# A reordered prologue: zero products, weights split in pieces, four combinations side by side

## The reference

```
mod = (silu(c) @ wmod).reshape(4, 6, 1, 512)      # sa, ca, ga, sb, cb, gb
h   = layernorm(x) * (1 + ca) + sa
q   = h @ Wq.T                                    # 32 heads of 128
k_r = h @ Wkr.T                                   # rotary part of the keys, 8 heads
c_kv = h @ Wdk.T                                  # 512 wide
k_c, v = c_kv @ Wupk.T, c_kv @ Wupv.T             # the keys' rest and the values
q, k = rope(q), rope(k)
x   = x + ga * (softmax(mask(q k^T / sqrt(128))) v @ Wo.T)
h   = layernorm(x) * (1 + cb) + sb
x   = x + gb * (h * w_sum + w_top8 @ expert_bias) # router softmax, best 8 of 64
```

## Time and profile before

| | |
|---|---|
| median of 3 runs | 1451.65 us (1451.25 to 1452.85) |
| profiled execution | 1450.45 us, span in the profile 1449.2 us |
| TensorE | busy 1428.9 us, 99% |
| VectorE | busy 1152.3 us, 80% |
| POOL | busy 1023.7 us, 71% |
| ScalarE | busy 1009.4 us, 70% |

### The profile page before, as it was taken

One profiled execution on the slowest core, in us unless ns is written; L12 is line 12 of the kernel. 1 busy time (PEld: TensorE's weight loads), 2 busy tenths in 40 slices (PEclk: granted clock), 3 DMA queues, 4 the chain that ended last, 5 costly groups with the idle time before them and its releaser, 6 DMA issues.

```text
span 1449.2 us, 24714 instructions
## 1 busy us (share of the span) xinstructions
PE 1428.9 (99%) x7150; PEld 1209.3 (83%) x7150; DVE 1152.3 (80%) x3542; ACT 1009.4 (70%) x2391; POOL 1023.7 (71%) x805
## 2 busy tenths in 40 slices
PE   7999999999999999999999999999999999999997
PEld 7888888888888888888888888888888888888886
DVE  6697777777777777778777777777879989988876
ACT  5687767667767666676777677676667676776674
POOL 3777877667767666776767687667588888886662
PEclk9999999999999999999999999999999999999999
DMA  9488668766766876686588658759888889889871
GB/s 321 152 248 257 211 179 228 223 213 185 209 208 197 229 202 211 189 246 178 170 229 243 205 182 225 191 161 268 238 234 265 262 286 281 265 267 268 270 233 61
DMA packets 215158, 322.05 MB, mean 222 GB/s; under 512 B 42512, under 2 KB 132464, under 8 KB 215024
## 3 DMA queue, kind: packets, MB, share of 16 engines
q1 hardware_dynamic: 214736, 320.39, 74.1%
q10 hardware_dynamic: 288, 0.07, 0.0%
HBM read 179.43 MB, written 140.95 MB: 221 GB/s over the span
## 4 chain that ended last, share of the span: by engine, by line
PE 87%; DVE 5%; POOL 3%; DMA 2%; issue 2%; ACT 1%; SPq 0%; DVEq 0%; ACTq 0%
PE bank_s L642 22%; PE bank_o L804 22%; PE bank_pv L766 14%; PE bank_s L708 13%; PE bank_s L674 6%; PE bank_s L659 5%; PE bank_s L705 1%; PE bank_s L704 1%; POOL PT_lo L1891 1%; DMA PT_raw<-blocks 1%; PE bank_s L613 1%; PE bank_s L868 1%; DVE blocks L1529 1%; DVE y L1581 0%; DMA wc_scratch<-wc_out 0%
## 5 line engine op out<-in xcount | busy, mean ns | idle before, releaser
L1891 POOL TENSOR_TENSOR PT_lo<-PT_raw,PT_hi 128x640 fp32r<-128x640 f32 x246 | 382.6, 1577 | 29.0 <-ACT PT_hi L1152 29.0
L1138 ACT ACTIVATE probs<-probs,row_inv 128x512 f32<-128x512 f32 (+3 forms) x512 | 257.6, 553 | 192.7 <-DVE row_inv L1512 192.6
L1879 POOL TENSOR_TENSOR rot_c<-rot_c,rot_s 128x512 f32<-128x512 f32 x128 | 167.8, 1311 | 251.5 <-DVE rot_s L1469 251.5
L1131 ACT ACTIVATE probs<-probs,row_min 128x384 f32<-128x384 f32 (+3 forms) x512 | 281.6, 552 | 47.9 <-DVE row_min L1505 47.7
L1529 DVE STREAM_TRANSPOSE blocks<-probs 128x384 f32<-128x384 f32 x508 | 213.9, 447 | 20.3 <-ACT probs L1138 13.0
L708 PE MATMUL bank_s<-kT_both,qT_hi 128*128 128x512 f32 (+2 forms) x768 | 215.1, 341 | 1.2 <-issue 0.6
L1505 DVE CUSTOM_DVE_ANT_0 probs<-bank_s,mask 128x512 f32<-128x512 f32 (+2 forms) x384 | 205.3, 552 | 0.3
L1884 POOL TENSOR_TENSOR qT_lo<-rot_c,qT_hi 128x512 fp32r<-128x512 f32 x128 | 166.6, 1301 | 51.7 <-ACT qT_hi L1113 51.0
L804 PE MATMUL bank_o<-wo_lo,OT_hi 128*128 128x512 f32 x496 | 195.0, 393 | 0.2 <-DVE rot_s L1469 0.2
L804 PE MATMUL bank_o<-wo_hi,OT_hi 128*128 128x512 f32 x496 | 193.4, 390 | 0.0
L804 PE MATMUL bank_o<-wo_hi,OT_lo 128*128 128x512 f32 x496 | 193.0, 389 | 0.0
(11 more groups left out here) (311 smaller groups left out, 3204.3 us busy)
## 6 DMA issues: line engine op xcount, KB each, us to landing
blocks<-blocks SPq DMA_DIRECT2D x127, 640.0 KB, 3.7
PT_raw<-blocks SPq DMA_DIRECT2D x500, 160.0 KB, 3.9
stage<-in_wq SPq DMA_DIRECT2D x32, 256.0 KB, 5.2
vblocks<-kv_raw SPq DMA_DIRECT2D x32, 256.0 KB, 5.4
kv_raw<-vblocks SPq DMA_DIRECT2D x128, 64.0 KB, 2.2
stage<-in_wo SPq DMA_DIRECT2D x32, 256.0 KB, 5.0
split_wq<-wq_hi SPq DMA_DIRECT2D x32, 256.0 KB, 5.4
split_wq<-wq_lo SPq DMA_DIRECT2D x32, 256.0 KB, 5.6
```

The costliest lines, as they stand in the source:

```text
L1131: ins = act.activation(row(t, qt), row(t, qt), ACT.Exp, bias=row_min[m][:, qt:qt + 1], scale=-1.0, accum_out=row_sum[m][:, qt:qt + 1])
L1138: ins = act.activation(row(t, qt), row(t, qt), ACT.Copy, scale=row_inv[t % 2][:, qt:qt + 1])
L1879: pool.tensor_tensor(rot_c[:], rot_c[:], rot_s[:], ALU.add).then_inc(pool_a, 1)
L1891: pool.tensor_tensor(lo[:, at], raw_of(t)[:, at], hi[:, at].bitcast(F32), ALU.subtract).then_inc(pool_t, 1)
```

## The change

Six things change, all ahead of step 5:

1. VectorE clears `kv_rot` first, and TensorE multiplies it with itself 13 times (`warm_up`), with a result nobody reads.
2. The first part of the up-weights is rounded and subtracted in four pieces, each with its piece of Wdk (`split_first_weights`), where it was one instruction for the whole part.
3. Combinations 0 to 3 are made together in four banks (`combine_first`): the hi·hi products of each piece as soon as it is rounded, then the others. Before, they came one after another.
4. `FIRST_CHUNKS` begins with wk in place of wq0, and the six subtractions on POOL are placed anew.
5. On TensorE `k_proj(0)` and `q_proj(0)` stand ahead of what they followed: `k_proj(0)` is ahead of `transpose_h(4)` and `(5)`, `q_proj(0)` ahead of `transpose_h(6)`, `q_proj(1)` ahead of `transpose_h(7)`.
6. The loads and stores on SP and the lists of ScalarE, VectorE and POOL follow that.

```
-FIRST_CHUNKS = ["wq0", "wk", "wq1", "wv", "wq2", "wq3"]
+FIRST_CHUNKS = ["wk", "wq0", "wq1", "wv", "wq2", "wq3"]
+SIDE_BY_SIDE = ["s3", "s2", "pv", "o3"]
+COMBINE_BANKS = SIDE_BY_SIDE + ["s3", "s2"] * ((SOON - CH) // 2) + ["o0", "o1"] * ((COMBINED - SOON) // 2)
+WARM_UPS = 13
 ...
+            def warm_up():
+                pe.wait_ge(dve_pro, ROT_CLEAR)
+                for _ in range(WARM_UPS):
+                    pe.matmul(bank["s1"][:, 0:P], kv_rot[:, 0:P], kv_rot[:, P:2 * P], start=True, stop=True)
+            def combine_first():
+                for m in range(CH):
+                    pe.wait_ge(split_w, 2 * m + 2)
+                    for i in range(CH):
+                        pe.matmul(bank[COMBINE_BANKS[i]][:, 0:2 * KVC], wdk[0][:, m, i * P:(i + 1) * P],
+                                  wup_hi[0][:, m, :], start=(m == 0), stop=False)
+                for i in range(CH):
+                    for m in range(CH):
+                        if i == 0:
+                            pe.wait_ge(split_lo, 2 * m + 2)
+                        for k, (down, up) in enumerate(((wdk[0], wup_lo[0]), (wdk[1], wup_hi[0]))):
+                            mm = pe.matmul(bank[COMBINE_BANKS[i]][:, 0:2 * KVC], down[:, m, i * P:(i + 1) * P],
+                                           up[:, m, :], start=False, stop=(m == CH - 1 and k == 1))
+                    mm.then_inc(pe_comb, 1)
 ...
-                if i >= 2:
-                    pe.wait_ge(act_comb, i - 1)
+                pe.wait_ge(act_comb, i - 3 if i < CH + 2 else i - 1)
 ...
-            combine(0)
-            combine(1)
-            combine(2)
+            warm_up()
+            combine_first()
             modulation(0)
-            combine(3)
+            combine(4)
             modulation(1)
             transpose_h(0)
             transpose_h(1)
             transpose_modulation()
-            combine(4)
             combine(5)
 ...
+            combine(9)
+            pe.wait_ge(pool_h, CH)
+            pe.wait_ge(act_comb, SIDE_BY_SIDE.index("o3") + 1)
+            k_proj(0)
             transpose_h(4)
             transpose_h(5)
-            combine(9)
-            pe.wait_ge(pool_h, CH)
-            k_proj(0)
-            transpose_h(6)
-            pe.wait_ge(pool_h, CH)
             pe.wait_ge(dve_pro, MODT)
             q_proj(0)
+            combine(10)
+            transpose_h(6)
+            q_proj(1)
             transpose_h(7)
-            combine(10)
-            q_proj(1)
             combine(11)
 ...
+            def split_first_weights():
+                act.wait_ge(d_wup[0], 16)
                 for m in range(CH):
+                    act.activation(wup_hi[0][:, m, :], wup_in[0][:, m, :], ACT.Copy).then_inc(split_w, 1)
                     act.wait_ge(d_wdk[m], 16)
                     act.activation(wdk[0][:, m, :], wdk_in[:, m, :], ACT.Copy).then_inc(split_w, 1)
```

More of the change, by code:

```diff
@@ L1276, in scalar_program @@
             combine(1)
-            normalise_x(0)
             combine(2)
             combine(3)
+            normalise_x(0)
+            combine(4)
             split_h(0)
-            combine(4)
+            split_h(1)
             split_up(2)
-            split_first(0)
             combine(5)
-            split_h(1)
+            combine(6)
             split_h(2)
-            combine(6)
-            normalise_x(1)
             split_h(3)
             combine(7)
+            split_first(0)
             split_first(1)
+            normalise_x(1)
             combine(8)
+            combine(9)
+            normalise_x(2)
+            k_split(0)
             split_first(2)
             split_h(4)
-            combine(9)
             split_h(5)
-            normalise_x(2)
-            split_up(3)
-            split_h(6)
-            k_split(0)
-            split_first(3)
-            split_first(4)
             combine(10)
             q_split(0)
+            split_up(3)
+            split_first(3)
+            split_h(6)
+            split_first(4)
+            q_split(1)
+            combine(11)
             split_h(7)
-            combine(11)
-            q_split(1)
             split_first(5)
@@ L1737, in vector_program @@
             modulate_h(0)
+            modulate_h(1)
             statistics(1)
-            modulate_h(1)
             modulate_h(2)
@@ L1743, in vector_program @@
             statistics(2)
-            modulate_h(4)
-            modulate_h(5)
             dve.wait_ge(dve_pro, ROT_CLEAR)
@@ L1748, in vector_program @@
             k_rope(0)
+            modulate_h(4)
+            modulate_h(5)
+            q_rope(0)
             modulate_h(6)
-            dve.wait_ge(d_const, 64)
-            q_rope(0)
-            modulate_h(7)
             statistics(3)
             q_rope(1)
+            modulate_h(7)
             split_up(3)
@@ L2016, in pool_program @@
             split_h(0)
+            split_h(1)
             statistics(1)
-            split_piece(FIRST_CHUNKS[0], 0, 0)
-            split_h(1)
             split_h(2)
             split_h(3)
+            split_piece(FIRST_CHUNKS[0], 0, 0)
             split_piece(FIRST_CHUNKS[1], 1, 1)
             statistics(2)
+            k_rope(0)
+            k_split(0)
+            split_h(4)
             split_piece(FIRST_CHUNKS[2], 0, 2)
-            split_h(4)
+            q_rope(0)
+            q_split(0)
             split_h(5)
-            k_rope(0)
+            split_piece(FIRST_CHUNKS[3], 1, 3)
+            q_rope(1)
+            q_split(1)
             split_h(6)
-            q_rope(0)
-            k_split(0)
-            q_split(0)
-            split_piece(FIRST_CHUNKS[3], 1, 3)
             split_piece(FIRST_CHUNKS[4], 0, 4)
-            q_rope(1)
             split_h(7)
-            q_split(1)
             split_piece(FIRST_CHUNKS[5], 1, 5)
```

50 lines of the change are left out of this document (24 added, 26 removed).

## The result

The changed kernel takes 1457.49 us (median of 7 runs, 1456.66 to 1458.23), against 1452.85 us (7 runs, 1451.25 to 1453.89) for the kernel before, measured beside it: a ratio of 1.0034, interval 1.0025 to 1.0044. It is slower by 3.6 to 6.4 us. A second measurement gave 1457.7 against 1451.93, ratio 1.0040 (1.0027 to 1.0052).

What follows compares the result with a forecast made beforehand. TensorE was taken as the bound, busy 1428.9 of 1449.2 us. scores(1) at 61.6 against 57.50 gave +4.1, less 0.5 given back: 1451.65 + 3.6 = 1455.25 us, range 1449.8 to 1457.8.

Steps and rivals of the forecast that it cites:

- the likeliest case: The forecast itself: TensorE loses its lead waiting for POOL's query weights, +3.6 us, 1455.25 us; chance 0.48.
- the clock rival: Rival: the second wait, ahead of q_proj(2), drops TensorE to 1.2 GHz; +5.3 us, 1457.0 us; chance 0.17.
- The start: TensorE's first products: first pair ready at 6.3 us, modulation(0) done at 16.4, a lead of 4.3 us.
- POOL's chain for sequence 0: POOL's small instructions get quicker as VectorE's subtraction starts near 14.1 us; ScalarE normalises from 16.2, not 17.06.
- `combine(7)`: TensorE waits 1.4 us, to about 27.05, for the bank ScalarE copies out after rounding the third up-weights.
- POOL from `k_rope(0)` to wq2: POOL's 12 instructions, roundings and contention, from 38.3 us, make wq2 ready at 56.7 us; before, 52.1.
- the contention with `split_up(3)`: POOL's q_rope(1) to q_split(1) meets VectorE's fourth split_up: 1.0 us taken, bounds 0 and 1.5.
- The waits: TensorE waits for POOL's subtracted query weights: 1.9 us for wq1 and 4.4 us for wq2.
- Given back: Between 60 and 140 us, existing TensorE waits absorb 0.5 us of the delay, within 0 to 0.8.
- The rival of a carried lead: Rival: q_proj(1) and q_proj(2) don't wait for POOL and the 3.0 us lead goes through; 1448.7 us; chance 0.20.
- The rival of a delay given back: Rival: beyond 60 us part of the delay comes back; about +1 us, 1452.7 us; chance 0.15.

Runs made afterwards that it cites:

- POOL early: The changed kernel with POOL's subtractions of wq1 and wq2 moved earlier, and ScalarE's roundings and the load of wq1 placed to feed them: 1449.15 us, ratio 0.9982.
- the one moved step: The changed kernel with POOL's subtraction of wq2 moved directly behind that of wv, and its rounding on ScalarE moved too: 1452.64 us, ratio 1.0008.
- the wait is filled: The changed kernel with 14 unread products of 128 columns between scores(0) and q_proj(2) on TensorE: 1457.57 us, ratio 1.0043.
- keys first: The changed kernel with ScalarE's copy of combine(5) ahead of the third up-weights' rounding, and normalise_x(2) behind the rounding of h(5): 1456.72 us, ratio 1.0037.
- waits removed: POOL early with further steps of ScalarE, VectorE and POOL reordered against the waits at combine(7) and ahead of scores(0): 1450.09 us, ratio 0.9987.

## Why the prediction was right, and where it was not

The forecast was 1455.25 us, slower by 3.6; the measured ratio is slower by 4.9 us (3.6 to 6.4). The median of 1457.49 is 0.3 us inside the stated range, but above the likeliest case's 1453.9 to 1456.6 and nearest to the clock rival's 1457.0; 1.2 us of it is that the kernel before came out at 1452.85 and not 1451.65. The step that carried the forecast, that TensorE's lead ends at POOL's subtraction of wq2, is shown by POOL early and by the one moved step. Term by term:

- **The start.** The first real product came at 6.80, not 6.3. Some 0.35 us of that are ScalarE's: its first pair of pieces was rounded at 6.59, for it began at 5.49 and took 1.10 us where 0.91 was taken. The zero products account for 0.15 at most: they took 5.4 to 5.6 us, all of them at the low pace (the row has 26 instructions for 13 products), where 4.5 was taken with a part at the high pace. The bounds were 0.8 to 8.3. They raised the clock as assumed. `modulation(0)` started at 15.89 and ended near 16.9, 0.5 us late.
- **POOL's chain for sequence 0.** The step failed that it gets quicker because VectorE's subtraction moves away from it: `split_up(1)` began at 14.59, not 14.1, and POOL's instruction beside it took 2.47 us where the undisturbed ones take 1.04. `normalise_x(0)` began at 17.57, not 16.2 and later than before (17.06).
- **`combine(7)`.** The wait was foreseen and is 0.97 us (1.4 said), but at 27.93 and not 27.05: the up-weights were rounded from 26.02, where 25.1 to 25.5 was taken. Issuing the transfer 3.55 us earlier gained 0.25, not 1 us. With it `k_proj(0)` came at 34.30 instead of 33.35: 0.95 us of the lead overestimated. (The two transposes behind it are 0.8 us, not 0.9.)
- **POOL from `k_rope(0)` to wq2.** Predicted 56.7 - 38.3 = 18.4 us, measured 57.80 - 39.53 = 18.3. Inside it two terms were off and cancelled: the wait for the keys' rounding was 1.04 us (behind `normalise_x(2)` on ScalarE) where 0.75 was taken, and the contention with `split_up(3)` 0.7 us (`q_split(1)` 2.00, `q_split(0)` 1.29) where 1.0 was taken. VectorE paid as well, 2.39 us against 1.88 in the earlier trace rows. By the Trainium skill, GPSIMD Engine Reference (Specifications), VectorE contends with GpSimd when its instruction has two SBUF inputs or runs in a 2-port mode; the trace agrees, since the POOL instructions beside VectorE's `k_rope` and `q_rope`, which read PSUM, keep 1.25 to 1.30 us.
- **The waits.** 2.35 and 3.88 us were measured for 1.9 and 4.4 predicted.
- **The clock.** Set as a rival of 0.17 at +5.3 us, and it came true beside the forecast, in both traces of the changed kernel. `q_proj(2)` took 4.4 us instead of 2.75. This is the one term missing from the forecast; 1.4 us of it vanish when the wait is filled. Together with 1.25 us at the start of `q_proj(2)` it makes `scores(1)` 64.39 where 61.6 was said. By the Trainium skill, TensorE: Matmul & The Clock Gate (Part 1), idleness brings the low level back; the traces agree with it after 3.7 to 3.9 us, and of seven waits of 2.06 to 2.59 us at one place only that of 2.07 in keys first brought it back.
- **Given back.** 0.5 us was subtracted. The traces show nothing given back: `scores(4)` is 7.75 us late where `scores(1)` is 6.9, since it waits 0.81 us itself, for POOL's `k_split(1)`. The forecast's 3.6, 1.25 of late start, 1.6 of clock, these 0.5 and 0.85 more make 7.8, the trace's 7.75.

In the traces the loss is thus 7.7 us, beyond the forecast's 3.6 and beyond its range of its own, 2.2 to 4.9; in the timed medians 4.6 and 5.8. That the forecast looks nearly right in time is partly luck: it owes 2 to 3 us to the two profiled executions lying differently among their like, which the working could not see. The rival of a carried lead is refuted for the change as it stands; POOL early shows that it needs another order on POOL. The rival of a delay given back is refuted.

What stays open: why a wait of 2.07 us brought the low level and waits of 2.06 to 2.59 did not; and why `scores(4)` and the time disagree by up to 3 us. POOL early and waits removed start it 0.2 us and 0.05 us before the kernel before and are 2.6 and 1.9 us faster by their ratios, and behind its start the traces have between 1355.1 and 1358.2 us left. So which part of these gains in time belongs to the lead is not shown.

## What to carry to other kernels

When work is moved ahead on the busiest engine, write down for each helper engine the row of instructions between the inputs that became early and the outputs that are now wanted early: a helper at 71% of its time can still be the bound for 20 us, and one subtraction three steps too late made most of the loss. A lead reaches the end only if every chain behind it is early too: two orders gave 3 us of it back at `scores(4)`, at two different waits, before a third kept 2 of them. An instruction that waits at the head of a helper's queue for something not urgent (here a normalisation, in waits removed done at 64.3 us and first read near 76) is the first to move.
